# Choosing the tokens of the experts with each list on four partitions, counted by ScalarE

## The reference, cut to what matters

```python
xn = layernorm(x); s = attention(xn); g = silu(ffn(xn)); x = x + s * g      # layer 0, x is (2, 4096, 256)
xn = layernorm(x); s = state_space_scan(xn); g = silu(moe(xn)); x = x + s * g   # layer 1

def moe(hidden_states):                               # b = 2, s = 4096, 16 experts
    cap = int(s * 2.0 / 16)                           # 512
    logits = einsum('bsd,ed->bse', hidden_states, gate_w)
    scores = softmax(logits, axis=-1).transpose(0, 2, 1)
    topk_w, topk_idx = top_k(scores, cap)             # 512 of 4096 tokens for each of 32 lists
    x_tok = take_along_axis(hidden_states, topk_idx)  # and their gated feed-forward, times topk_w,
    ...                                               # added back by token, plus a shared expert
```

## Time and profile before

| | us |
|---|---|
| median of 3 runs | 5014.06 (5011.34 to 5014.55) |
| the profiled execution, its own time | 5004.19 |
| its span | 5002.3 |
| its granted TensorE clock, mean | 0.944 |
| busy: TensorE, VectorE, ScalarE, GpSimd | 4413.1, 3570.6, 2524.3, 2539.3 |

### The profile page before, as it was taken

One profiled execution on the slowest core, in us unless ns is written; L12 is line 12 of the kernel. 1 busy time (PEld: TensorE's weight loads), 2 busy tenths in 40 slices (PEclk: granted clock), 3 DMA queues, 4 the chain that ended last, 5 costly groups with the idle time before them and its releaser, 6 DMA issues. The chain is left out here.

```text
span 5002.3 us, 63736 instructions
## 1 busy us (share of the span) xinstructions
PE 4413.1 (88%) x22534; PEld 3233.9 (65%) x22534; DVE 3570.6 (71%) x5059; ACT 2524.3 (50%) x4773; POOL 2539.3 (51%) x1838
## 2 busy tenths in 40 slices
PE   8899999968999999789999757789999989999982
PEld 7788888857888888666666424456666656666540
DVE  5466666654666666358878888887887888888895
ACT  6444444445444444466665412266656666666642
POOL 3122222232222200156656427788888888998870
PEclk9999999989999999899999758899999999999996
DMA  2122222220222200234434211355555555565556
GB/s 87 34 75 85 84 85 84 76 80 32 69 85 84 81 22 22 67 115 139 133 124 135 94 52 60 99 173 163 177 179 160 171 168 174 179 180 160 166 155 277
DMA packets 270465, 573.15 MB, mean 115 GB/s; under 512 B 37185, under 2 KB 156226, under 8 KB 270146
## 3 DMA queue, kind: packets, MB, share of 16 engines
q1 hardware_dynamic: 245570, 535.51, 32.0%
q0 software_dynamic: 24576, 33.57, 3.8%
HBM read 446.16 MB, written 122.81 MB: 114 GB/s over the span
## 5 line engine op out<-in xcount | busy, mean ns | idle before, releaser
L1533 POOL TENSOR_TENSOR scan_drive_sb<-scan_b_wide_sb,scan_du_sb 128x1024 f32<-128x1024 f32 x512 | 1295.9, 2561 | 447.7 <-DVE scan_h_sb L1444 446.1
L1444 DVE TENSOR_TENSOR_SCAN scan_h_sb<-decay_bank,scan_state_sb,scan_drive_sb 128x512 f32<-128x512 f32 x896 | 1116.2, 1268 | 86.2 <-ACT decay_bank L1768 85.5
L1629 PE MATMUL y_bank<-scan_ch_sb,identity_sb 128*128 128x512 f32 x2048 | 1076.5, 621 | 0.4 <-DVE scan_temp_sb L1457 0.4
L1768 ACT ACTIVATE decay_bank<-scan_delta_sb,a_neg_sb 128x512 f32<-128x512 f32 x1024 | 701.2, 687 | 542.3 <-DVE scan_h_sb L1444 539.7
L1451 DVE TENSOR_TENSOR scan_ch_sb<-c_pair,scan_h_sb 128x1024 f32<-128x1024 f32 x512 | 615.2, 1202 | 117.3 <-PE c_pair L1620 116.6
L958 PE MATMUL ybank<-v_low_hi_lo_sb,pt_hi_b_sb 128*128 128x384 f32 x2048 | 663.0, 358 | 22.0 <-DVE pt_lo_b_sb L838 15.6
L838 DVE TENSOR_TENSOR pt_lo_b_sb<-pt,pt_hi_b_sb 128x512 fp32r<-128x512 f32 x512 | 353.0, 690 | 413.9 <-ACT pt_hi_b_sb L1001 413.9
L959 PE MATMUL ybank<-v_low_hi_lo_sb,pt_lo_b_sb 128*128 128x256 f32 x2048 | 572.2, 279 | 0.0
L992 ACT ACTIVATE p_b_sb<-scores,softmax_cols_b_sb 128x1024 f32<-128x1024 f32 x256 | 286.0, 1117 | 550.9 <-DVE softmax_cols_b_sb L832 411.0
L1001 ACT ACTIVATE pt_hi_b_sb<-pt 128x512 fp32r<-128x512 f32 x512 | 306.2, 598 | 413.6 <-PE pt L946 413.6
L1620 PE MATMUL c_pair<-scan_cc_sb,select_state_sb 128*128 128x512 f32 x1024 | 379.7, 453 | 138.6 <-DVE scan_ch_sb L1451 137.7
(11 more groups left out here) (312 smaller groups left out, 9866.5 us busy)
## 6 DMA issues: line engine op xcount, KB each, us to landing
scan_b_wide_sb<-b_scratch SPq DMA_DIRECT2D x512, 512.0 KB, 3.8
w_hi_scratch<-split_hi_sb SPq DMA_DIRECT2D x51, 512.0 KB, 2.8
w_lo_scratch<-split_lo_sb SPq DMA_DIRECT2D x51, 512.0 KB, 4.1
expert_hi_sb<-w_hi_scratch SPq DMA_DIRECT2D x48, 512.0 KB, 5.3
expert_lo_sb<-w_lo_scratch SPq DMA_DIRECT2D x48, 512.0 KB, 6.3
x_b_sb<-x SPq DMA_DIRECT2D x16, 512.0 KB, 4.0
g_scratch<-g_out_b_sb SPq DMA_DIRECT2D x16, 512.0 KB, 3.2
split_raw_sb<-WgT SPq DMA_DIRECT2D x16, 512.0 KB, 5.4
```

What stands on the lines that cost most here:

```text
L1444: e.tensor_tensor_scan(k.h[i % H_BUFFERS][:, j, :], k.decay_banks[S % DECAY_BANKS][:, :], k.drive[i % DRIVE_BUFFERS][:, j, :], start, ALU. ...
L1533: e.tensor_tensor(k.drive[i % DRIVE_BUFFERS][:, :, :], k.b_wide[i % B_BUFFERS][:, :, :], k.du[c % 2][:, :].unsqueeze(1).broadcast_to([P, P ...
L1629: e.matmul(k.y_bank[:, :], consts.identity[:, :], k.ch[i % CH_BUFFERS][:, j, :], start=(n == 0), stop=(n == STATES - 1)).then_inc(k.s_y, 1)
L1768: e.activation(k.decay_banks[S % DECAY_BANKS][:, :], k.delta[c % 2][:, :], ACT.Exp, scale=wt.a[:, n:n + 1]).then_inc(k.s_decay, 1)
```

## The change

The 30 rounds, the ranks and the slots are done with each list on four partitions of 1024 tokens (a partition for each quarter of a sequence).

- TensorE turns the scores into that layout by 8 transposes, ScalarE copies them to SBUF (`by_list`).
- A round: VectorE makes minus the trial in one column of 128 values; ScalarE takes the sign of score minus trial over 128x1024 with a running sum (`accum_out`), TensorE adds the four sums of each list with a 0/1 matrix (`k.group`), VectorE compares with `SIGN_SUM` and sets the bit. The comparison and the sum over 128x1024 on VectorE are gone.
- One more count (`ties`) corrects the value where it lies exactly on a trial.
- Ranks: one running sum over 1024 columns for each mask, with the sums of the partitions before it from a one-column matmul (`k.below`). Slots are made in that layout and turned back by 16 transposes and four copies on ScalarE (`row`, `col`).
- GpSimd makes `k.group` in two selections and `k.below` in one, and no longer fills `k.reset`.
- `CHOOSE_STEPS` is 103.

```diff
--- before.py
+++ after.py
 PICK_BITS = 3
-PICK_RANKS = PICK_BITS + 4 * SCORE_BITS
-PICK_LISTS = PICK_RANKS + 17
+PICK_TIES = PICK_BITS + 2 * SCORE_BITS
+PICK_RANKS = PICK_TIES + 3
+PICK_SLOTS = PICK_RANKS + 9
+PICK_LISTS = PICK_SLOTS + 5
+
+
+QUARTERS = 4
+QUARTER = SEQ // QUARTERS
+TURNS = QUARTER // P
+
+SIGN_SUM = 2 * CAPACITY - 1 - SEQ
+
+NEXT_FLOAT = 1.25 * 2.0 ** -24
+
+TIES_STEP = 1 + SCORE_BITS
+BACK_STEP = TIES_STEP + 4
+LISTS_STEP = BACK_STEP + 1
...
-CHOOSE_STEPS = SCORE_BITS + 1 + 4 + 1 + 4 + 1 + 1 + 2 * (LISTS + 1) + 1
+CHOOSE_STEPS = LISTS_STEP + 2 * (LISTS + 1) + 1
+
...
+def turns(t, half):
+
+    return flat(t).rearrange("p (m k) -> p m k", k=TURNS)[:, :, half * GT:(half + 1) * GT]
...
+    def back(half, what, to):
+        fills.wait_filled(w, what, half)
+        turned = fills.bank(what, half).rearrange("p (k m) -> p m k", k=GT)
+        e.activation(turns(to, half), turned, ACT.Copy).then_inc(fills.emptied(what, half), 1)
+
     def choose():
-        yield from no_steps(CHOOSE_STEPS - 1 - 2 * LISTS)
+        yield
+        for half in range(2):
+            fills.wait_filled(w, "by_list", half)
+            e.activation(flat(k.equal)[:, half * BANK:(half + 1) * BANK], fills.bank("by_list", half), ACT.Copy).then_inc(fills.emptied("by_list", half), 1)
+        for half in range(2):
+            fills.wait_emptied(w, "by_list", half)
+        for r in range(SCORE_BITS):
+            w.wait_ge(k.s_pick, PICK_BITS + 2 * r + 1)
+            if r > 0:
+                fills.wait_filled(w, "bit", r - 1)
+            e.activation(flat(k.tmp), flat(k.equal), ACT.Sign, bias=k.trial[:, :].bitcast(F32), accum_out=k.count[:, :]).then_inc(k.s_signs, 1)
+            yield
+        yield from no_steps(BACK_STEP - TIES_STEP)
+        w.wait_ge(k.s_pick, PICK_LISTS - 1)
+        for half in range(2):
+            back(half, "row", k.above)
+        yield
+        for half in range(2):
+            back(half, "col", k.rank)
+        yield from no_steps(CHOOSE_STEPS - 1 - 2 * LISTS - LISTS_STEP)
...
+        by_quarter = lambda t: t[:, :].rearrange("p (l q) -> p l q", q=QUARTERS)
+        e.affine_select(out=by_quarter(k.group), in_=by_quarter(consts.ones), compare_op=ALU.is_gt, fill=0.0,
+                        base=1, pattern=[[-QUARTERS, LISTS], [0, QUARTERS]], channel_multiplier=1).then_inc(k.s_made, 1)
+        w.wait_ge(k.s_made, 1)
+        e.affine_select(out=by_quarter(k.group), in_=by_quarter(k.group), compare_op=ALU.is_gt, fill=0.0,
+                        base=QUARTERS, pattern=[[QUARTERS, LISTS], [0, QUARTERS]], channel_multiplier=-1).then_inc(k.s_made, 1)
+        w.wait_ge(k.s_made, 2)
+        e.affine_select(out=k.below[:, :], in_=k.group[:, :], compare_op=ALU.is_gt, fill=0.0,
                         base=0, pattern=[[1, P]], channel_multiplier=-1).then_inc(k.s_made, 1)
-        e.memset(k.reset[:, :, :], 1.0).then_inc(k.s_made, 1)
...
     def choose():
-        over_lists = lambda ap: ap.unsqueeze(2).broadcast_to([P, LISTS, TILES])
...
+        A, E, T, R = (flat(t) for t in (k.above, k.equal, k.tmp, k.rank))
+        add_up = consts.ones[:, 0:1].broadcast_to([P, QUARTER])
+        last = R[:, QUARTER - 1:QUARTER]
...
+        yield
         for r in range(SCORE_BITS):
-            bit, at = SCORE_BITS - 1 - r, PICK_BITS + 4 * r
+            bit, at = SCORE_BITS - 1 - r, PICK_BITS + 2 * r
             w.wait_ge(k.s_pick, at)
-            e.tensor_scalar(k.trial[:, :], k.bits[:, :], 1 << bit, None, ALU.bitwise_or).then_inc(k.s_pick, 1)
-            w.wait_ge(k.s_pick, at + 1)
-            e.tensor_tensor(all_of(k.tmp), all_of(k.scores), over_lists(k.trial[:, :].bitcast(F32)), ALU.is_ge).then_inc(k.s_pick, 1)
-            w.wait_ge(k.s_pick, at + 2)
-            e.tensor_reduce(k.count[:, :], all_of(k.tmp), AX_X, ALU.add).then_inc(k.s_pick, 1)
+            e.tensor_scalar(k.trial[:, :], k.bits[:, :], (1 << bit) - (1 << 31), None, ALU.bitwise_or).then_inc(k.s_pick, 1)
...
-            e.tensor_scalar(k.step[:, :], fills.bank("bit", r)[:, 0:LISTS], float(CAPACITY), float(1 << bit),
...
+        found = k.bits[:, :].bitcast(F32)
+        w.wait_ge(k.s_pick, PICK_TIES)
+        e.tensor_scalar(T, E, found, None, ALU.is_gt).then_inc(k.s_pick, 1)
+        w.wait_ge(k.s_pick, PICK_TIES + 1)
+        e.tensor_reduce(k.count[:, :], T, AX_X, ALU.add).then_inc(k.s_pick, 1)
+        yield
+        fills.wait_filled(w, "ties")
+        e.tensor_scalar(k.tie[:, :], fills.bank("ties")[:, 0:1], float(CAPACITY), NEXT_FLOAT, ALU.is_ge, ALU.mult).then_inc(fills.emptied("ties"), 1)
+        fills.wait_emptied(w, "ties")
+        e.scalar_tensor_tensor(k.value[:, :], found, k.tie[:, :], found, ALU.mult, ALU.add).then_inc(k.s_pick, 1)
         w.wait_ge(k.s_pick, PICK_RANKS)
-        e.tensor_tensor(all_of(k.above), all_of(k.scores), threshold, ALU.is_gt).then_inc(k.s_pick, 1)
-        e.tensor_tensor(all_of(k.equal), all_of(k.scores), threshold, ALU.is_equal).then_inc(k.s_pick, 1)
-        yield
+        e.tensor_scalar(A, E, k.value[:, :], None, ALU.is_gt).then_inc(k.s_pick, 1)
+        e.tensor_scalar(E, E, k.value[:, :], None, ALU.is_equal).then_inc(k.s_pick, 1)
         w.wait_ge(k.s_pick, PICK_RANKS + 1)
-        e.tensor_reduce(k.count[:, :], all_of(k.above), AX_X, ALU.add).then_inc(k.s_pick, 1)
+        e.tensor_reduce(k.count[:, :], A, AX_X, ALU.add).then_inc(k.s_pick, 1)
+        w.wait_ge(k.s_pick, PICK_RANKS + 2)
+        e.tensor_tensor_scan(R, add_up, E, 0.0, ALU.mult, ALU.add).then_inc(k.s_pick, 1)
...
+        e.tensor_scalar(k.need[:, :], fills.bank("need")[:, 0:1], -1.0, float(CAPACITY), ALU.mult, ALU.add).then_inc(fills.emptied("need"), 1)
...
+        e.scalar_tensor_tensor(k.room[:, :], fills.bank("before", "equal")[:, 0:1], -1.0, k.need[:, :],
+                               ALU.mult, ALU.add).then_inc(fills.emptied("before", "equal"), 1)
...
+        e.scalar_tensor_tensor(T, R, k.room[:, :], E, ALU.is_le, ALU.mult).then_inc(k.s_pick, 1)
+        w.wait_ge(k.s_pick, PICK_RANKS + 5)
+        e.tensor_tensor(A, A, T, ALU.add).then_inc(k.s_pick, 1)
+        w.wait_ge(k.s_pick, PICK_RANKS + 6)
+        e.tensor_tensor_scan(R, add_up, A, 0.0, ALU.mult, ALU.add).then_inc(k.s_pick, 1)
+        e.tensor_scalar(T, A, -2.0 * SEQ, 2.0 * SEQ - 1.0, ALU.mult, ALU.add).then_inc(k.s_pick, 1)
+        yield
+        fills.wait_filled(w, "before", "above")
+        e.tensor_copy(k.offset[:, :], fills.bank("before", "above")[:, 0:1]).then_inc(fills.emptied("before", "above"), 1)
+        fills.wait_emptied(w, "before", "above")
+        w.wait_ge(k.s_pick, PICK_RANKS + 8)
+        e.scalar_tensor_tensor(T, R, k.offset[:, :], T, ALU.add, ALU.add).then_inc(k.s_pick, 1)
+        at, slot, half = PICK_SLOTS, A.bitcast(I32), R.bitcast(I32)
+        w.wait_ge(k.s_pick, at)
+        e.tensor_copy(slot, T).then_inc(k.s_pick, 1)
...
+        e.tensor_scalar(half, slot, 5, None, ALU.logical_shift_right).then_inc(k.s_pick, 1)
...
+        e.tensor_copy(E, half).then_inc(k.s_pick, 1)
...
+        e.tensor_scalar(half, slot, COLS32 - 1, None, ALU.bitwise_and).then_inc(k.s_pick, 1)
...
+        e.tensor_copy(T, half).then_inc(k.s_pick, 1)
+        yield
+        yield
+        for half in range(2):
+            fills.wait_emptied(w, "row", half)
+            fills.wait_emptied(w, "col", half)
...
+    def from_counts(by, count, *key):
         bank = fills.take(w, *key)
-        e.matmul(bank[:, 0:LISTS], consts.ones[:, :], k.count[:, :], start=True, stop=True).then_inc(fills.filled(*key), 1)
+        e.matmul(bank[:, 0:1], by[:, :], count, start=True, stop=True).then_inc(fills.filled(*key), 1)
...
+    def by_token(what, src):
+        for half in range(2):
+            bank = fills.take(w, what, half)
+            for j in range(GT):
+                turn = half * GT + j
+                turned = e.transpose(bank[:, j * P:(j + 1) * P], flat(src)[:, turn * P:(turn + 1) * P], consts.identity[:, :])
+            turned.then_inc(fills.filled(what, half), 1)
...
     def choose():
-        flat = lambda t: t[:, :, :].rearrange("p l t -> p (l t)")
+        w.wait_ge(k.s_scores, ALL_GROUPS)
+        for half in range(2):
+            bank = fills.take(w, "by_list", half)
+            for j in range(GT):
+                turned = e.transpose(bank[:, j * P:(j + 1) * P], turns(k.scores, half)[:, :, j], consts.identity[:, :])
+            turned.then_inc(fills.filled("by_list", half), 1)
+        yield
...
         for r in range(SCORE_BITS):
-            total(PICK_BITS + 4 * r + 3, "bit", r)
+            w.wait_ge(k.s_signs, r + 1)
+            from_counts(k.group, k.count[:, :], "bit", r)
             yield
...
+        w.wait_ge(k.s_pick, PICK_TIES + 2)
+        from_counts(k.group, k.count[:, :], "ties")
+        yield
+        w.wait_ge(k.s_pick, PICK_RANKS + 3)
+        from_counts(k.group, k.count[:, :], "need")
+        w.wait_ge(k.s_made, 3)
+        ends = flat(k.rank)[:, QUARTER - 1:QUARTER]
```

(12 more changed lines are left out.)

98 lines of the change are left out of this document (22 added, 76 removed).

## The result

| | before | after |
|---|---|---|
| median, us | 5014.31 (4 runs, 5011.34 to 5016.5) | 4962.6 (4 runs, 4957.59 to 4963.18) |
| ratio | 1 | 0.9895 (95% interval 0.9878 to 0.9912) |
| the profiled execution, its own time | 5004.19 | 4962.26 |
| its span | 5002.3 | 4960.5 |
| its granted TensorE clock, mean | 0.944 | 0.948 |

The change is faster by 51.7 us, where 60 were forecast. The two profiled executions differ by 42 only: the scan's first recurrence started at 2175.8 in the one of before and at 2184.1 in the one of after, and in the thirteen profiled executions of the change and its variants it lay between 2178.5 and 2185.6, in code that the change doesn't touch. So I compare stretches, each measured from one start in the trace to the next.

A forecast was written before the change was run, and what follows sets the result against it. VectorE was taken to bound the rounds (91% busy). Start 2.4, rounds 105, ranks and slots 33 and tail 8.6 gave 149 against 209 us, 60 less: 4954 us from the median 5014.06, range 4934 to 4984.

The forecast's parts named there:

- The bound of before: In the choice's 30 rounds: VectorE sets the pace, busy 144.8 of 158.5 us, 91%.
- Start, +2.4: Ahead of the first trial: one recurrence and one product of the scan now stand there, 2.4 us more.
- Rounds, 105: The 30 rounds of the choice: 105 us against 158.5, with ScalarE's pass in the chain.
- `bits` waits 1.1 here: In 12 rounds with a recurrence alone: `bits` meets GpSimd's work and waits 1.1 us, making 3.6 us each.
- The projections' stall: In the rounds: two scan projections stand ahead of counts on TensorE, 4.0 us each, now uncovered, 8 us.
- Ranks and slots, 33: Ranks and slots, up to the first one-hot mask: 33 us against 50.7.
- Tail, +8.6: End of the scan: five recurrences and two products fewer done in the choice are paid back there, 8.6 us.
- same work, nothing taken: Lists (197.8 us) behind the choice: same work, no change of time put into the sum.
- given back later: Rival, lists and experts: experts meet the scan 5 steps earlier in its chunk, 30 us lost, 4984; chance 0.08.
- TensorE at its lower clock: Rival, rounds: TensorE takes over, 0.5 us in each of 30 rounds, 15 us, 4969; chance 0.15.
- Better cover: Rival, rounds: clock rises at once, GpSimd's work falls beside ScalarE's pass, 16 us less, 4938; chance 0.11.
- Table loads: Rival, rounds: a load at each sign-decay change, 46 at 1.59 us, 73 us, 5027, slower; chance 0.03.

The follow-up runs named there:

- Six idle steps: The changed kernel with six empty steps of the experts' thread just ahead of the lists: 4947.77 us, ratio 0.9867.
- 24 pairs made by hand: The changed kernel with a one-column GELU ahead of each sign, forcing table loads between sign and decay: 4991.31 us, ratio 0.9949.
- a rate of 0.5: The changed kernel with `pace.rate` 0.5 in rounds and ranks, and `bits` reading one operand from SBUF, one from PSUM: 4920.73 us, ratio 0.9811.
- a rate of 1.0 and one read less: The changed kernel with `pace.rate` 1.0 in rounds and ranks, and `bits` reading one operand from SBUF, one from PSUM: 4925.54 us, ratio 0.9823.

## Why the prediction was right, and where it was off

**The bound of before.** Right: VectorE set the rounds. With its two large operations back on VectorE the rounds are 140.6 us, without them 100.5.

**Start, +2.4.** Measured +2.1.

**Rounds, 105.** Measured 100.5, by partly other terms, and so in part by luck. The pass was taken at 1.2 us and takes 1.25 (2847.40 to 2848.65 in ScalarE's timeline). The count behind it, taken at 0.67, came in 0.47 (to 2849.12), and the small operations and handovers, 0.64, in 0.56: 2.28 us for the shortest round.

| rounds | forecast | measured |
|---|---|---|
| 7 with neither | 2.5 each, 17.5 | 2.5 each (six of them), 17.4 |
| 12 with a recurrence | 3.6 each, 43 | 2.45 each, 29.5 |
| 11 with both | 3.0 each, 33 | 3.89 each, 42.8 |
| projections and the rest, above these | 11 | 10.9 |

The step that failed is "`bits` waits 1.1 here", in the rounds with a recurrence alone. The meeting with GpSimd stayed where it had been before the change, in the round with the product itself, and only eight `bits` met it. The rows of before show it already: the `bits` of 1.29 us at 2841.80 ends a round with a product. The two errors, 13.5 and 9.8 us, nearly cancel. The projections' stall was right: VectorE waits 4.10 us before `scan_out` at 2888.91 and 6.62 before a step at 2899.15.

**Ranks and slots, 33.** Measured 32.1. The running sums (twice 1.22 expected, 2.28) and the way back (2.5 us taken, one wait of 2.16) held. The meetings with GpSimd held in size, 2.2 us against 2.6, but not in place: I had put them on two single-input passes, and they fell on a small operation with two SBUF inputs (1.29 us) and on a two-input pass (2.35 where 1.22 was taken). These are VectorE's rows of after, against the earlier trace rows:

```profile
2943.40 1.29 DVE L2320 SCALAR_TENSOR_TENSOR value_sb<-bits_sb,tie_sb 128x1 f32<-128x1 f32 x1
...
2947.19 2.28 DVE L2327 TENSOR_TENSOR_SCAN rank_sb<-ones_sb,equal_sb 128x1024 f32<-128x1024 f32 x1
...
2958.86 2.35 DVE L2348 SCALAR_TENSOR_TENSOR tmp_sb<-rank_sb,offset_sb,tmp_sb 128x1024 f32<-128x1024 f32 x1
...
2968.20 1.28 DVE L1444 TENSOR_TENSOR_SCAN scan_h_sb<-decay_bank,scan_state_sb,scan_drive_sb 128x512 f32<-128x512 f32 x1 [2.16 <-ACT rank_sb L2111]
...
2971.12 0.68 DVE L2372 TENSOR_TENSOR onehot_left_sb<-above_sb,iota_f_sb 128x512 f32<-128x512 f32 x1
```

**Tail, +8.6.** Measured +7.7. Five recurrences and two products at the prediction's own prices (1.18 and 1.1) are 8.1; 2.5 whole items count half a product too many.

**Lists and experts: "same work, nothing taken".** This is the step that failed. The work is the same, the time isn't: 14.2 us more, which I had only as a rival ("given back later", a few us either way likely). It is what separates the forecast 60 from the measured 51.7. Six idle steps give all of it back, and behind the mask VectorE and GpSimd then execute the same instructions in the same order as before (1555 and 955 rows of the two traces, in pairs). The other terms together came to 66.8 us of gain, 6.6 more than forecast.

**The rivals.** TensorE at its lower clock: no, the clock rose to 0.64 and the rounds took 100.5 us where this rival had 120. Better cover: partly, the rounds were 4.5 us better. Table loads: none, 30 signs of 1147 to 1150 ns stand among the decays without one. For this pair the advice of the Trainium skill (page "ScalarE: Activation LUTs", section "Table sets: the hidden batching unit") to batch by set has nothing to save. My price for that rival, 73 us, was also too high: 24 pairs made by hand cost 32.8 us in the rounds, and the kernel stayed 24 us faster than before. I had put every load into the chain and at 1.59 us, and about half of their time went into ScalarE's waits.

## What to carry to other kernels

When two threads share in-order queues, a stage that becomes shorter moves everything behind it against the other thread; give that a range of its own (here 0 to 14 us of 1750, and 18 at a rate of 0.5), and try a few idle steps before judging the change. When an engine is relieved, ask at once what else could be done in the room it now has: the relief was worth 52 us as made, and another rate of merging the threads 27 to 43 more (with the alignment that each rate brought). A wait that only appears beside another engine's instruction (0.16 us in one round, 1.06 in the next) is worth one edit of an operand's place.

## What the runs showed of the hardware

- More work made TensorE's stretch no longer. In the rounds it had 150 matmuls in 66.69 us at a granted clock of 0.64, and 178 in 64.58 us at 0.82 in the run with a rate of 1.0 and one read less. TensorE's timeline of the kernel after shows the step within one round: two matmuls of `c_pair` take 1.20 us at 2840.48 and 0.70 at 2846.65, after the engine had worked from 2840.48 almost without a gap to 2845.5. The granted clock is 0.50 from 2840.40 to 2845.50 and 1.00 from 2846.40 to 2849.50:

```profile
2840.48 1.20 PE L1620 MATMUL c_pair<-scan_cc_sb,select_state_sb 128*128 128x512 f32 x2
...
2846.65 0.70 PE L1620 MATMUL c_pair<-scan_cc_sb,select_state_sb 128*128 128x512 f32 x2
```

- The count of one column, with two loads of a 128x128 matrix, follows the clock too, loads and all. Behind a wait it takes 0.58 us at the lower clock (2891.37) and 0.38 at the higher (2846.41); its two loads take 0.50 us together against 0.30. At the lower clock it takes 0.43 where it stands right behind the scan's matmuls (2843.18).
- Writing a step of one column to PSUM and reading it back costs what SBUF costs on VectorE (164 and 155 ns against 154 and, where it met nothing, 158 to 159), so the detour around the meeting with GpSimd is all but free.
